# Inverse deviations of the expert layers taken from the attention's variance, the chain moved behind a unit's combination, one weight split a step

## What is computed

```python
x = x + _L0_attn_ref(_layernorm(x), ...)
x = x + _L0_ffn_ref(_layernorm(x), ...)      # four layers of _moe_layer on y = _layernorm(x)
def _moe_layer(x, rw, rb, g, b, w1, b1, w2, b2):
    logits = jnp.einsum('bsh,he->bse', x, rw) + rb          # four experts, the best two
    ...
    xhat = xc * jax.lax.rsqrt((xc * xc).mean(axis=-1, keepdims=True) + EPS)
    xe = xhat[None] * g[:, None, None, :] + b[:, None, None, :]
    h = gelu(einsum('ebsh,ehf->ebsf', xe, w1) + b1);  y = einsum('ebsf,efh->ebsh', h, w2) + b2
    return jnp.einsum('bse,ebsh->bsh', comb, x[None] + y)
```

## Time and profile before

| | |
|---|---|
| median of 3 runs | 1382.77 us (1380.51 to 1383.1) |
| profiled execution | 1380.24 us, its span 1378.5 us |
| mean granted TensorE clock | 0.97 |
| PE, DVE, ACT, POOL busy | 1270.3, 1203.2, 1128.8, 714.0 us |

### The profile page before, as it was taken

How to read it: one execution, slowest core, us unless ns; L and a number is a source line. 1 busy time by engine, 2 the same in 40 slices (tenths; PEclk the granted TensorE clock), 3 DMA queues, 4 the chain that set the end, 5 groups by cost and what they waited for, 6 DMA issues and landing times. The chain is left out here.

```text
span 1378.5 us, 41462 instructions
## 1 busy us (share of the span) xinstructions
PE 1270.3 (92%) x15611; PEld 966.0 (70%) x15611; DVE 1203.2 (87%) x3492; ACT 1128.8 (82%) x1931; POOL 714.0 (52%) x559
## 2 busy tenths in 40 slices
PE   5898999999997689997889979999999999999998
PEld 3576778777776578954567657777777777776776
DVE  4799989999998678977899979998999999999986
ACT  3598999999996656766899968888888888888886
POOL 7276777777776864542334333344333344444343
PEclk9999999999998679999999999999999999999999
DMA  5985676676663279820000000000000000000000
GB/s 157 240 217 156 191 184 183 188 189 183 191 183 86 49 198 209 216 53 1 2 2 2 2 1 2 2 2 2 2 2 2 2 2 2 2 10 17 10 17 17
DMA packets 196269, 109.41 MB, mean 79 GB/s; under 512 B 89740, under 2 KB 194028, under 8 KB 196076
## 3 DMA queue, kind: packets, MB, share of 16 engines
q1 hardware_dynamic: 122032, 84.65, 22.1%
q10 hardware_dynamic: 74044, 22.17, 7.3%
HBM read 67.62 MB, written 39.03 MB: 77 GB/s over the span
## 5 line engine op out<-in xcount | busy, mean ns | idle before, releaser
L1649 POOL TENSOR_TENSOR gl<-gf,gh 128x1024 f16<-128x1024 f32 x128 | 290.6, 2270 | 461.7 <-ACT gh L1671 461.7
L1666 ACT ACTIVATE gf<-pair,b1c 128x512 f32<-128x512 f32 x512 | 329.5, 680 | 77.1 <-PE pair L1846 76.9
L1863 PE MATMUL pair<-w2p,gh 128*128 128x128 f16 x4096 | 356.9, 219 | 4.3 <-DVE hs L1745 2.6
L1863 PE MATMUL pair<-w2p,gl 128*128 128x128 f16 x2048 | 349.7, 219 | 0.0
L1846 PE MATMUL pair<-xh,w1p 128*128 128x512 f16 x1024 | 328.3, 382 | 7.3 <-DVE w1p L1046 7.3
L405 POOL TENSOR_TENSOR pl<-p,ph 128x1024 f16<-128x1024 f32 x128 | 273.1, 2134 | 116.0 <-ACT ph L462 115.9
L1863 PEld LDWEIGHTS pair<-w2p,gh 128*128 128x128 f16 x4096 | 317.5, 98 | 20.8 <-DVE hs L1745 3.1
L1671 ACT ACTIVATE gh<-gf 128x1024 f16<-128x1024 f32 x256 | 270.6, 1057 | 23.6 <-ACT gf L1666 0.4
L1731 DVE SCALAR_TENSOR_TENSOR gl<-gf,gh 128x1024 f16<-128x1024 f32 x128 | 164.0, 1281 | 42.0 <-ACT gh L1671 41.5
L1863 PEld LDWEIGHTS pair<-w2p,gl 128*128 128x128 f16 x2048 | 200.3, 98 | 0.0
L1846 PE MATMUL pair<-xl,w1p 128*128 128x512 f16 x512 | 195.7, 382 | 0.0
(11 more groups left out here) (252 smaller groups left out, 2458.0 us busy)
## 6 DMA issues: line engine op xcount, KB each, us to landing
KS<-k_parts_dram SPq DMA_DIRECT2D x64, 384.0 KB, 4.5
k_parts_dram<-kh SPq DMA_DIRECT2D x64, 256.0 KB, 3.3
cx<-in_ctx_dram ACTq DMA_DIRECT2D x30, 512.0 KB, 4.7
k_parts_dram<-kl SPq DMA_DIRECT2D x64, 128.0 KB, 3.6
w1p<-in_L_ffn_w_dram SPq DMA_DIRECT2D x8, 512.0 KB, 6.0
w2p<-in_L_ffn_w_dram SPq DMA_DIRECT2D x8, 512.0 KB, 8.0
QS<-q_parts_dram ACTq DMA_DIRECT2D x128, 24.0 KB
K<-k_parts_dram SPq DMA_DIRECT2D x8, 384.0 KB
```

The costliest lines, as they stand in the source:

```text
L1649: pool.tensor_tensor(gl[u.m2][:, 0:h, :], gf[u.m2][:, 0:h, :], gh[u.m2][:, 0:h, :], ALU.subtract).then_inc(d_loP, 1)
L1666: act.activation(gf[u.m2][:, c, :], hb[c][:, :], ACT.Gelu, scale=1.0 / WS, bias=b1c[:, u.step.expert(u.e), c]).then_inc(d_g, 1)
L1863: last = pe.matmul(yb[v.m2][:, t * D:(t + 1) * D], g[:, c, t * P:(t + 1) * P], w2p[:, le, part, c, :].rearrange("p a h -> p (a h)"), start ...
```

## The change

Layer 0's second inverse deviation is worked out from the attention's variance instead of from hs: the variance of (x - mean) * r is var * r * r. `expert_scale` (15 small instructions, all of a slice's tiles at once) does this into rsE and rrE, and `normalise_first` makes xc straight from xs. So layer 0 has no bn_stats and no chain in its steps. `tokens_high` and `tokens_low` (xh and xl of block 0) move into the first Block; so does PE's transpose of xc, ahead of the last tile's output. The last eight tiles' moments move to steps 1 and 2 of the second Block, and hs of tiles 16 to 31 is written by DVE (`attended_late`) at e = 3 of steps 2 to 5. In layers 1 to 3 `deviations` is parted: moments stay ahead of xl, the chain stands behind the combination of e = 1. hs += xs in the last layer goes to POOL. There is one split a step, in steps 1 to 12, and PE waits for each expert's split by itself.

```diff
+        vE, rsE, rwE, rrE = (sb(whole, f"rsE_{i}", [P, NT], F32) for i in range(4))
+        xh = [sb(whole, f"xh{i}", [P, 4 * P], F16) for i in range(2)]
+        xl = [sb(whole, f"xl{i}", [P, 4 * P], F16) for i in range(2)]
...
+        SCALED = HEAD + 2 * RSTD_STEPS + 4
+        LATE_R = SCALED + NT - HEAD + RSTD_STEPS
+        LATE_SCALED = LATE_R + RSTD_STEPS + 3
+        def expert_scale(dve, own, base):
+            dve.wait_ge(e_ln, base)
+            dve.scalar_tensor_tensor(vE[:, own], mv3[:, own, 1], 1.0, rs3[:, own], ALU.mult, ALU.mult).then_inc(e_ln, 1)
+            dve.wait_ge(e_ln, base + 1)
+            dve.scalar_tensor_tensor(vE[:, own], vE[:, own], 1.0, rs3[:, own], ALU.mult, ALU.mult).then_inc(e_ln, 1)
+            dve.wait_ge(e_ln, base + 2)
+            inverse_deviation(dve, seed, rsE[:, own], rwE[:, own], rt3[:, own], vE[:, own], e_ln, base + 2)
+            dve.scalar_tensor_tensor(rrE[:, own], rs3[:, own], 1.0, rsE[:, own], ALU.mult, ALU.mult).then_inc(e_ln, 1)
+        def normalise_first(dve, n):
+            dve.wait_ge(e_ln, SCALED if 4 * n + 4 <= HEAD else LATE_SCALED)
+            wait(dve, d_xT, n)
+            for k in range(4):
+                t = 4 * n + k
+                dve.tensor_scalar(xc[:, k, :], xs[:, t, :], mv3[:, t, 0:1], rrE[:, t:t + 1],
+                                  ALU.subtract, ALU.mult).then_inc(d_x, 1)
+        def tokens_high(act, n):
+            act.wait_ge(d_xT, n + 1)
+            act.activation(xh[n % 2][:, :], bank[6][:, :], ACT.Copy).then_inc(d_xh, 1)
+        def tokens_low(dve, n):
+            dve.wait_ge(d_xh, n + 1)
+            dve.tensor_tensor(xl[n % 2][:, :], bank[6][:, :], xh[n % 2][:, :], ALU.subtract).then_inc(d_xl, 1)
...
-                                for t in range(8):
+                                for t in range(4):
                                     attended(act, t)
                             if at == (NBLK, 0):
                                 act.activation(warm[:, :], gain[:, 0:1], ACT.Gelu)
+                                for t in range(4, 8):
+                                    attended(act, t)
+                            if at == (NBLK, 1):
+                                tokens_high(act, 0)
                                 high_weights(act, 2)
-                            if at == (NBLK, 1):
-                                for t in range(8, 12):
-                                    attended(act, t)
                             if at == (NBLK, 2):
...
+                            if at == (7, 3):
+                                expert_scale(dve, slice(0, HEAD), HEAD + RSTD_STEPS + 1)
                             if at == (NBLK, 0):
-                                dve.wait_ge(d_hs, 8)
-                                for k in range(8):
-                                    dve.bn_stats(st8[:, k, :], hs[:, k, :]).then_inc(d_ln, 1)
-                                dve.wait_ge(d_ln, 8)
-                                for k in range(8):
-                                    dve.bn_aggr(mv8[:, k // 4, k % 4, :], st8[:, k, :]).then_inc(d_ln, 1)
-                            if at == (NBLK, 1):
-                                flat = lambda r: r[:, :, :].rearrange("p i k -> p (i k)")
-                                dve.wait_ge(d_ln, 16)
-                                inverse_deviation(dve, seed, flat(rs8), flat(rw8), flat(rt8),
-                                                  mv8[:, :, :, 1].rearrange("p i k -> p (i k)"), d_ln, 16)
-                                for k in range(4):
-                                    dve.tensor_scalar(xc[:, k, :], hs[:, k, :], mv8[:, 0, k, 0:1], rs8[:, 0, k:k + 1],
-                                                      ALU.subtract, ALU.mult).then_inc(d_x, 1)
-                            if at in ((7, 3), (NBLK, 1)):
-                                le = (7, NBLK).index(at[0])
-                                dve.wait_ge(e_b1, le + 1)
-                                low_weights(dve, le)
-                    def attended_late():
-                        b = slice(HEAD, NT)
-                        done = HEAD + RSTD_STEPS + 1
-                        for t in range(HEAD, NT):
-                            dve.bn_aggr(mv3[:, t, :], st2[:, t, :]).then_inc(e_ln, 1)
-                        dve.wait_ge(e_ln, done + NT - HEAD)
-                        inverse_deviation(dve, seed, rs3[:, b], rw3[:, b], rt3[:, b], mv3[:, b, 1], e_ln, done + NT - HEAD)
-                        dve.scalar_tensor_tensor(nb3[:, b], mv3[:, b, 0], -1.0, rs3[:, b], ALU.mult, ALU.mult).then_inc(e_ln, 1)
+                                normalise_first(dve, 0)
+                                for le in range(2):
+                                    dve.wait_ge(e_b1, le + 1)
+                                    low_weights(dve, le)
+                            if at == (NBLK, 2):
+                                tokens_low(dve, 0)
...
                                               stop=(le == LE - 1)).then_inc(e_b1, 1)
+                            if at == (NBLK, 1):
+                                pe.wait_ge(d_x, 4)
+                                pe.wait_ge(c_oc, NT)
+                                for k in range(4):
+                                    last = pe.transpose(bank[6][:, k * P:(k + 1) * P], xc[:, k, :], ident[:, :])
+                                last.then_inc(d_xT, 1)
...
+                        if u and f and final and e == 0:
+                            blk = slice(4 * f.block, 4 * f.block + 4)
+                            pool.wait_ge(d_x, 4 * f.n + 4)
+                            pool.tensor_tensor(hs[:, blk, :], hs[:, blk, :], xs[:, blk, :], ALU.add).then_inc(d_sum, 1)
...
+                    def late_deviations():
+                        own = slice(HEAD, NT)
+                        for t in range(HEAD, NT):
+                            dve.bn_aggr(mv3[:, t, :], st2[:, t, :]).then_inc(e_ln, 1)
+                        dve.wait_ge(e_ln, SCALED + NT - HEAD)
+                        inverse_deviation(dve, seed, rs3[:, own], rw3[:, own], rt3[:, own], mv3[:, own, 1], e_ln, SCALED + NT - HEAD)
+                    def attended_late(n):
+                        dve.wait_ge(e_ln, LATE_R if 4 * n + 4 > HEAD else HEAD + RSTD_STEPS + 1)
+                        for t in range(4 * n, 4 * n + 4):
+                            dve.tensor_scalar(hs[:, t, :], xs[:, t, :], mv3[:, t, 0:1], rs3[:, t:t + 1],
+                                              ALU.subtract, ALU.mult).then_inc(d_hs, 1)
...
                         at = (u.step.n, e) if u and isinstance(u.step.n, int) else None
-                        opening = at is not None and at[0] == 0
                         if u and f and e == 0:
-                            normalise(f, final)
-                        if u and third and e == 1 and not opening:
-                            deviations(third)
-                        if f and e == 1:
-                            dve.wait_ge(d_xh, f.n + 1)
-                            dve.tensor_tensor(xl[f.m2][:, :], tbk[:, :], xh[f.m2][:, :], ALU.subtract).then_inc(d_xl, 1)
+                            if f.layer == 0:
+                                normalise_first(dve, f.n)
+                            else:
+                                normalise(f)
+                        if third and e == 1 and third.layer:
+                            moments(third)
+                        if u and f and e == 1:
+                            tokens_low(dve, f.n)
                         if u:
                             low_half(u)
                         if at == (0, 0):
                             low_weights(dve, 2)
                             weigh(u.step)
-                        if opening and e == 2:
-                            deviations(third)
                         if f and e == 2:
                             route(f)
                         if v:
-                            combine(v, final)
+                            combine(v)
+                        if third and e == 1 and third.layer:
+                            deviations(third)
                         if u and e == 3:
                             add_bias(u.step)
                         if at == (0, 1):
                             low_weights(dve, 3)
+                        if at == (1, 2):
+                            late_deviations()
+                        if at == (2, 2):
+                            expert_scale(dve, slice(HEAD, NT), LATE_R)
+                        if u and e == 3 and 2 <= u.step.n < 6:
+                            attended_late(u.step.n + 2)
                         if u and f and e == 3:
                             weigh(f)
                     dve.memset(c16[:, :, :, :].rearrange("p t g e -> p (t g e)"), 0.0).then_inc(d_c16, 1)
                     dve.wait_ge(d_c16, 1)
-                    steps(dve, unit, low_weights, (2, 3), lead=True)
+                    steps(dve, unit, low_weights, 3, lead=True)
...
```

(9 more changed lines are left out.)

120 lines of the change are left out of this document (48 added, 72 removed).

## The result

The changed kernel takes 1396.53 us (median of 4 runs, 1392.86 to 1400.57), the kernel before 1381.67 us (4 runs, 1380.51 to 1383.1). The ratio is 1.0112, 95% interval 1.0089 to 1.0136: **slower by 1.1%**, 14.9 us. The forecast was 1402 with a range of 1373 to 1414. The profiled execution took 1400.57 us, span 1398.8, at the upper end of its runs.

A forecast was written before the change was run, and what follows sets the result against it. PE, busy 92% of 1378.5 us, was taken as the bound, with DVE becoming it in steps with the moved chain. Gains of 28.3 us against costs of 48 gave +19.7 on 1380.24, or 1400; forecast median 1402, range 1373 to 1414.

The forecast's parts named there:

- The join: Between attention and first router: one chain replaces two chains, eight bn_stats and 16 aggregations, gaining 3.3 us (1.5 to 4.5).
- rival D: At the join: PE's last bias sums and b1r bound it, so it gains nothing; 1405 us, chance 0.06.
- The weights: PE no longer waits for all splits at once: 7.3 us, plus 2.2 of lowered clock, gaining 9.5 us.
- Layer 0's gains: Layer 0's steps: no chain in step 0's third unit, and waits for xl and xc gone, gaining 10.8 us.
- Layer 0's costs: Steps 1 to 5: late aggregations and chain 2.7, expert_scale step 5.6, attended_late 1.1 each; 12 us (5 to 22).
- The moved chain in plain steps: Steps 13 to 22: POOL's gl holds the moved chain and route, costing 1.1 us a step, 11 us (5 to 15).
- the walk: Instruction-by-instruction estimate of one steady step with the moved chain: z 2.1 us late, PE waiting 0.8, xc 0.3.
- Split steps: Steps 6 to 12, with chain and split on DVE: 2.4 us each, costing 17 us (12 to 19).
- The last layer: The addition of xs leaves DVE and xl stands ahead of the chain, so the 4.7 us of xl waits go.
- The price: Last layer: POOL's addition pushes POOL's next gl and DVE's behind it, seven steps at 1.2, 8 us (5 to 12).
- Rival B: Steps 6 to 29: the moved chain costs PE nothing, only splits cost; faster, 1371 us, chance 0.17.
- Rival C: Chain held but half absorbed, layer 0's cost at its lower bound; about level, 1381 to 1382 us, chance 0.07.

The follow-up runs named there:

- b1: Kernel before, with only PE's wait for each expert's weights at the first block of its layer, splits still two a step: 1374.58 us, ratio 0.9940.
- c2: Changed kernel with attended_late still on DVE but moved from unit 3 to unit 1, behind the combination: 1385.09 us, ratio 1.0032.
- a2: Changed kernel with layer 0's attended tiles 16 to 31 written by ACT at unit 1, not by DVE at unit 3: 1385.68 us, ratio 1.0021.
- a1: Changed kernel with the chain of layers 1 to 3 put back in front of xl: 1392.7 us, ratio 1.0064.
- b2: Kernel before, with only the last layer's addition of the attention's output moved to POOL: 1384.71 us, ratio 1.0010.
- d1: Changed kernel with the last layer's addition of the attention's output on DVE again, behind xc: 1402.13 us, ratio 1.0152.
- b3: Kernel before, with only the chain of layers 1 to 3 moved behind the first unit's combination: 1390.96 us, ratio 1.0059.

## Why the prediction was right, and where not

The direction, the mechanism and the total held: 1396.5 against 1402. The parts behind the total were sized less well.

- **The join**, 3.3 forecast: 4.2 us from the tile at (7, 3), inside the range of 1.5 to 4.5, and 1.3 more in stretch 0. The size held, the reason for it less: behind the last tile PE's bias sums and b1r end the join now, which the forecast had named as its lower end and as rival D. The first router came at 630.2, not at 627, because this execution's attention was 4 us late.
- **The weights**, 9.5: against the 22.27 us of a plain step the old stretch 7 lost 9.5. It is 8.9 us shorter now, since the split and the chain there take 0.6 back (counted again under the split steps), and alone, in b1, 8.2. Right.
- **Layer 0's gains**, 10.8: stretch 1 gives 3.8, and c2's stretches 5 and 6 (22.85 us) show what a step of the new layer 0 takes, one split included, when the late tiles cost nothing (a2, with them on ACT, has 22.86): against the 25.26, 24.51 and three of 23.50 us of before that is 6.0. Together 9.8, or 11.1 if stretch 0 is counted here and not at the join. Right.
- **Layer 0's costs**, 12 (5 to 22): **this step failed**. Against 22.85 us each, stretches 2 to 6 are 24.1 us longer. The deviations cost 5.9 instead of 2.7, the second scaling 4.5 instead of 5.6, and attended_late 4.6 three times instead of 1.1. The forecast put that last value between "not held" and "held", where the rows say held: 2.38 us for four instead of 1.11, then xc as well (3.07), which it had named only as the upper end, and a clock that falls behind each wait (1.6 us of the 4.6). Its own test asked whether steps 2 to 5 would take under 23 us; the stretches 3 to 6 took 27.3 to 27.6, so the term was too small, not too large.
- **The moved chain in plain steps**, 1.1 each, 11 us: **mis-sized**. It is 0.44 in stretches 15 to 22, and 3.1 us in the nine stretches 14 to 22 by a1. The hold is as forecast. But three chain instructions and five of the route were done before POOL began, where the walk had two and four. So z comes 1.8 us later against the router than in the earlier trace rows, instead of 2.1. By the walk's 1.4 us of slack that leaves 0.4, and PE begins 0.41 late where 0.8 was forecast; xc costs 0.18 instead of 0.3. And the walk took the old plain step for one without a wait; it lost 0.18 us for xl, which the move gives back.
- **Split steps**, 17 (12 to 19): 14.4 us by stretches 7 to 13 against 22.27 us each. The total fits, the pattern doesn't: 0.6, five times 1.7, and 5.4 in stretch 13, where xc fell under POOL's next gl once ACT had no split left. That the sum comes near 17 is luck: the six steps that are not stretch 13 cost 9.0, less than two thirds of what was put on them.
- **The last layer**, 4.7 gained and 8 paid: -0.8 us in all. The waits for xl, 4.7 us, are gone, but eight for the combination, 3.5 us, stand in their place. b2 refutes the gain as a term of its own, and d1 shows 4.3 us of it once the chain has moved. **The price failed**: POOL's addition does push POOL's next gl (b2), but a step of this layer takes 22.89 us, 0.2 more than the plain one of layer 2 and not 1.2. Nor does the chain's place make a difference beside the addition (a1 22.93 us a stretch, the changed kernel 22.90).
- **Rival B** is refuted by b3: the chain's move costs 8.2 us where it stands alone, some 2 of them in the wait for w1p. Rival D had the right bound and the wrong result: the join gained 4.2 us all the same. Rival C was nearer on the chain's price and further off on layer 0's.
- **A sum**: the bounds of the costs reach up to 15 + 19 + 12 + 22 = 68, not 63. The stated range did not hang on it.

So the good total is partly luck: about 12 us too little for layer 0, against 8 too much for the chain in plain steps, 3 for the split steps and 4 for the last layer.

## What to carry to other kernels

Where two engines exclude each other, an instruction's price is its place: the same four instructions cost 4.6 us a step in front of work that PE is about to need, and nothing in a gap of their own engine. Look for that gap by the idle time in front of each instruction, and check what is due right behind it. Take a hold that you have seen once at its full length and follow what it delays to the next turn of the other engine; late work can be caught by that turn as well, and then it pays twice. And ask of each part of a change by itself what it is worth: here the join and the weights' waits were good, and the places of the late tiles, of the chain and of the splits cost more than these gained.
